# A two-layer decoder on one core: more buffers for routed pages, and new engine orders for its last stage

## The chip, the cores and the metric
The kernel runs on one core of a Trainium2 chip. The time is that of the device for one execution, in microseconds (us); three runs of the kernel before gave 4082.57 (median), 4074.16 and 4083.14. One more execution was profiled. The core has five engines with instruction queues of their own: TensorE (PE), VectorE (DVE), ScalarE (ACT), GpSimd (POOL) and SyncE (SP), which only issues DMAs. Each runs its queue in order; semaphores tie them together.

## The reference
A decoder of two layers works on 4096 tokens (64 sequences of 64) with 128 features, all in float32. A second input of the same shape, the context, is used by the cross attentions.

```python
x = x + L0_attn(ln(x))           # delta rule attention, 4 heads      stage A
x = x + L0_xattn(ln(x), ctx)     # cross attention, 16 heads          stage B
x = x + L0_ffn(ln(x))            # 6 layers: local attention + FFN    stage C
x = x + L1_attn(ln(x))           # cosine attention, 16 heads         stage D
x = x + L1_xattn(ln(x), ctx)     # gated attention, 8 heads           stage E
x = x + L1_ffn(ln(x))            # mixture of experts                 stage F
```

In the last step each token is sent to 3 of 16 experts. An expert computes relu(x W1 + b1) W2 + b2 with a hidden width of 256; its result is weighted by the gate. The three results are added to the token.

## The kernel before
**Tiles and stages.** The tokens lie in 32 tiles of 128. Stage A+B ("ab"), stage C ("c") and stage D+E with the routing of F ("de") each run over the tiles as a software pipeline. A unit is one tile in one stage, and each unit consists of named items per engine. Stage C runs 6 layers over the 32 tiles, and after every four tiles a feed-forward unit C2; its last one (layer 5, group 7) ends the stage.

**Orders.** `DE_ORDER` holds for each engine the order of one slot. In `"G5 t4 T3"` the letters are the item and the last digit (base 36) is the lag: in slot n the engine runs item `G` of unit n-5, then `t` of unit n-4, then `T` of unit n-3. `schedule` gives every item a due time, BEGIN[stage][engine] + SLOT[stage] * (slot + place / items), and sorts all stages' items by it. So a stage's SLOT and BEGIN decide only how its items interleave with those of the neighbouring stages; within a stage the order is what `DE_ORDER` says. Waits are on semaphores and come from the data flow, whatever the order.

**Items of stage "de".** `st1`, `ag1`, `n1`, `r1`, `xn1` normalise the tile; `X1` transposes it, `J` is the projection to queries, keys and values; `sq`, `ln`, `lx`, `qn` scale them, `T` transposes, `s` (scores), `c0`, `c1` (clipping, DVE), `e0`, `e1` (exp, ACT), `p0`, `p1` (transposes), `u`, `n`, `t`, `w` (weighted values and output). The gated attention has `xc`, `g`, the gates' small items on DVE and ACT up to `cs`, `gb` (POOL, L1992), `G` (PE, two banks), `dm` and `mx` (DVE), `d2` (POOL, L1884), `ex` (ACT), `C` (DVE, L1369), `ct`, `av`, `hh` to `h4`, `h5`, `h6` (POOL) and `x`. The routing has `X3`, `g3`, `ti` to `cu` on DVE, `rk`, `gT`, `b2`, and `sc`: three scatters (POOL, L2021) of the tile's rows into the experts' lists in HBM (`xg`).

**Banks.** PE's results go to eight PSUM banks in turn (`take` in `build`); an item waits until whoever reads the bank's earlier result is done with it. `G`, `s` and `u` take two banks.

**Pages.** A page is 128 rows of one expert's list, with the expert's weights. There are 111. `FT` units (DVE) make tables of pages once 8, 12, 16, 20, 24, 28 and 32 tiles are routed; SP's `blocks` reads them and issues for each page two loads, of rows and their weights and targets (`XB`, 65 KB, L623) and of the expert's matrices (`FW`, 257 KB, L624). Page j runs through `T`, `h`, `o` on PE, `T`, `h` on ACT, `o` on DVE (result into `YB`), `zz` on POOL (scatter to `zg`, L2030). Pages 0 to 68 run inside the stage, three per slot from unit 9 on (`BT0`, `Bh0`, `Bo0` and so on; `Bz` on POOL); for earlier units PE runs filler matmuls (`fill`) in their places. Pages 69 to 110 come after it in the tail (`FB_ORDER`), then SP loads the results back and DVE and POOL add them.

**Places.** `XB` and `FW` have 8 places (`NXB`), `YB` has 4 (`NYB`). SP may load page j when PE has done `o` of page j-8 and the scatter of page j-8 has landed, since the scatter reads its targets from `XB`. DVE's `o` of page j waits for the scatter of page j-4.

**Activation tables.** ACT's `table` loads another set when an item needs it: gelu for the items `g0` to `g2` of C2, exponentials and logarithms for most of stage "de". Copies and squares need none.

Of the kernel before, what the change touches and what calls it, by code (L numbers as in the profile page):

```python
# [23 lines left out]
PAGES = (3 * TOK + NE * 127) // 128  # L24
XROWS = NE * CAP + PAGES * 128
ZROWS = 3 * TOK + (NE + PAGES) * 128
NXB, NYB = 8, 4
STEPS = [(t, 3 * t - 15) for t in range(8, NT, 4)] + [(NT, PAGES)]
# [4 lines left out]
def shape_constants():  # L33
# [14 lines left out]
    for k in range(5):  # L48
# [58 lines left out]
DE_ORDER = {  # L107
# [8 lines left out]
}  # L116
# [22 lines left out]
for _kind in "12":  # L139
# [7 lines left out]

SLOT = {"ab": 13.426, "c": 11.263, "de": 14.030, "fb": 1.2, "fc": 3.0}
BEGIN = {
    "ab": {"pe": 0.0, "act": -19.77, "dve": -27.0, "pool": -23.98},  # L150
    "c": {"pe": 448.83, "act": 425.56, "dve": 432.24, "pool": 458.45},
    "de": {"pe": 3221.92, "act": 3186.93, "dve": 3246.05, "pool": 3263.81},
}
# [93 lines left out]
def build(nc, din, out, stages=("A", "B", "C", "D", "E", "F"), depth=DEPTH):  # L247
    with ExitStack() as ctx:
# [11 lines left out]
        WB = sb("WB", [128, OF + 1066 + 128])  # L260
# [31 lines left out]
        tables = WB[0:1, 532:532 + 128 * len(STEPS)].bitcast(I32)  # L292
        FW = [WB[:, 1428 + 514 * p:1942 + 514 * p] for p in range(NXB)]
        XB = [WB[:, 5540 + 130 * p:5670 + 130 * p] for p in range(NXB)]
        YB = [WB[:, 6580 + 128 * p:6708 + 128 * p] for p in range(NYB)]
        XT = [WB[:, 7092 + 128 * p:7220 + 128 * p] for p in range(4)]
        HID = [WB[:, 7604 + 256 * p:7860 + 256 * p] for p in range(4)]
        xg = nc.dram_tensor("xg", (XROWS, 130), F32, kind="Internal").ap()
# [69 lines left out]
        names += ["wat0", "wat1", "wq", "wf", "out", "rt", "empty", "const", "rope", "ones", "blank", "prime", "half", "shift"]  # L368
        names += [f"xr{i}" for i in range(3)] + [f"bw{i}" for i in range(NXB)]
        names += [f"ys{i}" for i in range(NYB)] + ["lists", "seen"]  # L370
# [174 lines left out]
        def _(eng):  # L545
# [63 lines left out]
            def blocks():  # L609

                for s in qkv_free(depth - 1) + [uC2[(depth - 1, 7)].on("pe", "o")]:
                    w.wait_ge(*s)
                for k, u in enumerate(FT):
                    for p in range(3):
                        w.wait_ge(f"xr{p}", 48 * len(range(p, u.at["t"], 3)))
                    w.wait_ge(*u.on("dve", "v"))
                    for j in range(u.at["first"], u.at["n"]):
                        if j >= NXB:
                            w.wait_ge(*FB[j - NXB].on("pe", "o"))
                            w.wait_ge(f"ys{(j - NXB) % NYB}", 16 * ((j - NXB) // NYB + 1))  # L620
                        c = 128 * k + j - u.at["first"]
                        at = eng.value_load(tables[0:1, c:c + 1], min_val=0, max_val=XROWS - 128)
                        eng.dma_start(XB[j % NXB], xg[bass.ds(at, 128), :]).then_inc(sems[f"bw{j % NXB}"], 16)  # L623
                        eng.dma_start(FW[j % NXB], din["F_W"][bass.ds((at >> 12) * 128, 128), :]).then_inc(sems[f"bw{j % NXB}"], 16)  # L624

# [44 lines left out]
            w.wait_ge("rt", 16)  # L670
            for i in range(NXB):
                w.wait_ge(f"bw{i}", 32 * len(range(i, PAGES, NXB)))

# [4 lines left out]
        def _(te):  # L678
# [393 lines left out]
            def pe_fb(u, ph):  # L1072
                j = u.at["j"]
                for v, e, m in u.after[ph]:
                    w.wait_ge(*v.on(e, m))
                K, W = bank[u.bank[ph]], FW[j % NXB]
                if ph == "T":
                    w.wait_ge(f"bw{j % NXB}", 32 * (j // NXB + 1))
                    o = tr(K[:, 0:128], XB[j % NXB][:, 0:128])
                elif ph == "h":  # L1080
                    w.wait_ge(f"bw{j % NXB}", 32 * (j // NXB + 1))
                    w.wait_ge(*u.on("act", "T"))
# [12 lines left out]
        def _(se):  # L1095
# [241 lines left out]
            def act_fb(u, ph):  # L1337
                j = u.at["j"]
                K, W = bank[u.bank[ph]], FW[j % NXB]
                w.wait_ge(*u.on("pe", ph))  # L1340
# [4 lines left out]
                elif ph == "h":  # L1345
                    w.wait_ge(f"bw{j % NXB}", 32 * (j // NXB + 1))
                    if j >= 4:
# [9 lines left out]
        def _(ve):  # L1357
# [522 lines left out]
        def _(pe_):  # L1880
# [220 lines left out]
```

## Time and profile before

| what | value |
|---|---|
| runs, median of three | 4082.57 us |
| profiled execution | 4061.49 us |
| its span, first to last instruction | 4059.7 us |
| granted TensorE clock, mean | 0.961 of full |
| PE busy | 3798.1 us, 94% |
| DVE, ACT, POOL busy | 81%, 78%, 66% |
| stage "de" | about 3260 to 3940 us |
| tail: the last 42 pages, results, output | about 3940 to 4060 us |

The page cuts the span into 40 slices of 101.5 us. A digit of a slice is the busy share in tenths; in the line PEclk it is the clock granted to TensorE. In rows of instructions, `ps<-BIG` is what is written and read, and `[1.34 <-DVE BIG L1369]` says that the engine was idle for 1.34 us before it and that this instruction of VectorE ended the wait. `x8` is a count; a float32 matmul stands as two records. Most items share the lines of a few helpers (L682 matmul, L686 transpose, L1361, L1369, L1372 on DVE, L1099 and L1107 on ACT, L1884 on POOL), so they are told apart by their shapes and tiles.

### The profile page before, as it was taken

To read this page: it belongs to the slowest core of one execution; us is meant where nothing else is said; L and a number is where in the kernel's file an instruction comes from. 1 tells how busy PE (TensorE), PEld (TensorE's weight loads), DVE (VectorE), ACT (ScalarE), POOL (GpSimd) and SP (SyncE) were. 2 spreads that over 40 slices of the span, in tenths; PEclk is the share of its full clock that TensorE was granted. 3 is DMA by queue.
4 is the path that set the end of the run, shared out by engine and by line. 5 is a ranking of instruction groups with operands and counts; after the bars stand their busy time and mean duration, and the time that the engine had idled before them with its cause. 6 is when DMAs were issued, how large, how long until landed. Compare 5 with 4: busy or idle time off the path is not lost.

```text
span 4059.7 us, 143038 instructions
## 1 busy us (share of the span) xinstructions
PE 3798.1 (94%) x58268; PEld 2739.9 (67%) x58268; DVE 3285.5 (81%) x9302; ACT 3182.2 (78%) x9278; POOL 2692.5 (66%) x2319
## 2 busy tenths in 40 slices
PE   7999989999999999999999999999999978888873
PEld 5767756666676766766666766767666757667663
DVE  4666699998989999898889989898999847766642
ACT  3555579899999999999899999999998946656642
POOL 3444487887777777777777777777777714344444
PEclk9999999999999999999999999999999989977868
DMA  3000000000211111111201121111110000122246
GB/s 110 4 4 5 5 2 4 5 5 5 47 19 26 26 31 36 24 26 26 52 14 26 26 44 30 17 26 26 52 39 9 10 10 16 54 67 70 70 111 203
DMA packets 168664, 139.87 MB, mean 34 GB/s; under 512 B 37076, under 2 KB 148744, under 8 KB 167032
## 3 DMA queue, kind: packets, MB, share of 16 engines
q1 hardware_dynamic: 161384, 117.04, 12.9%
q0 software_dynamic: 6624, 13.68, 1.0%
q8 instruction: 461, 7.55, 0.8%
q14 instruction: 195, 1.60, 0.1%
HBM read 108.72 MB, written 57.23 MB: 41 GB/s over the span
## 4 chain that ended last, share of the span: by engine, by line
PE 71%; DVE 15%; ACT 8%; issue 4%; DMA 1%; POOL 1%; SPq 0%; DVEq 0%; another core or an unknown queue 0%; POOLq 0%; ACTq 0%
PE ps L682 55%; PE ps L686 16%; DVE BIG L1361 7%; ACT BIG L1107 5%; DVE sm L1372 3%; ACT BIG L1099 2%; DVE BIG L1369 1%; POOL sm L1887 1%; DVE sm L1361 1%; DMA zg<-WB 1%; DVE x_sb L1361 0%; DMA WB<-in_F_W 0%; DVE BIG L1503 0%; DVE sm L1543 0%; DVE WB L1365 0%
## 5 line engine op out<-in xcount | busy, mean ns | idle before, releaser
L1099 ACT ACTIVATE BIG<-ps 128x512 f32<-128x512 f32 (+5 forms) x2784 | 1450.8, 575 | 405.7 <-PE ps L686 235.4
L682 PE MATMUL ps<-WB,BIG 128*128 128x128 f32 (+2 forms) x6528 | 1682.1, 391 | 4.9 <-DVE BIG L1361 1.8
L1884 POOL TENSOR_TENSOR BIG<-BIG,sm 128x512 f32<-128x512 f32 (+1 forms) x864 | 1214.7, 1430 | 673.1 <-DVE sm L1543 305.2
L686 PEld LDWEIGHTS ps<-t_ident,BIG 128*128 128x128 f32 x5952 | 717.4, 144 | 486.2 <-issue 299.3
L1884 POOL TENSOR_TENSOR BIG<-BIG 128x512 f32<-128x512 f32 x776 | 972.8, 1280 | 87.4 <-DVE BIG L1361 72.4
L686 PE MATMUL ps<-t_ident,BIG 128*128 128x128 f32 x5952 | 914.4, 281 | 75.4 <-DVE BIG L1369 38.6
L682 PEld LDWEIGHTS ps<-WB,BIG 128*128 128x128 f32 (+1 forms) x6528 | 863.2, 192 | 174.3 <-issue 153.5
L1372 DVE TENSOR_REDUCE sm<-BIG 128x8 f32<-128x512 f32 (+5 forms) x1440 | 857.1, 623 | 6.9 <-ACT BIG L1107 5.2
L682 PEld LDWEIGHTS ps<-BIG 64*64 64x64 f32 (+2 forms) x37888 | 605.0, 128 | 321.6 <-issue 145.5
L682 PE MATMUL ps<-BIG 64*64 64x64 f32 (+4 forms) x37888 | 728.6, 222 | 62.8 <-ACT BIG L1107 18.1
L1107 ACT ACTIVATE BIG<-ps,sm 128x64 f32<-128x64 f32 (+1 forms) x3104 | 700.6, 394 | 37.7 <-DVE sm L1372 35.8
L1361 DVE TENSOR_TENSOR BIG<-ps,rc 128x512 f32<-128x512 f32 x768 | 525.6, 684 | 144.1 <-ACT BIG L1107 137.5
L1107 ACT ACTIVATE BIG<-ps 128x512 f32<-128x512 f32 (+1 forms) x832 | 496.2, 627 | 133.7 <-PE ps L682 119.0
L1361 DVE TENSOR_TENSOR BIG<-ps,rs 128x256 f32<-128x256 f32 x1536 | 570.9, 412 | 0.0
L1372 DVE TENSOR_REDUCE sm<-ps 128x8 f32<-128x512 f32 (+1 forms) x416 | 263.6, 643 | 113.0 <-PE ps L682 81.3
L1887 POOL TENSOR_TENSOR sm<-sm,halfn 128x1 f32<-128x1 f32 (+2 forms) x208 | 187.5, 902 | 206.2 <-DVE sm L1365 84.8
L682 PE MATMUL ps<-BIG,WB 128*128 128x512 f32 (+2 forms) x608 | 295.4, 577 | 1.4 <-ACT BIG L1107 1.4
L1099 ACT ACTIVATE ps<-t_bandm 128x512 f32<-128x512 f32 x384 | 233.4, 697 | 0.0
L1107 ACT ACTIVATE sm<-sm 128x32 f32<-128x32 f32 (+2 forms) x672 | 152.8, 232 | 65.0 <-DVE sm L1365 58.3
L682 PEld LDWEIGHTS ps<-BIG,WB 128*128 128x128 f32 (+2 forms) x608 | 104.2, 176 | 119.4 <-issue 83.5
L2030 POOL DMA_INDIRECT zg<-WB x111 | 109.3, 985 | 113.4 <-DVE WB L1365 83.3
L682 PE MATMUL ps<-WB 128*128 128x128 f32 (+1 forms) x926 | 170.3, 327 | 6.0 <-ACT WB L1107 3.0
(152 smaller groups left out, 3557.1 us busy)
## 6 DMA issues: line engine op xcount, KB each, us to landing
xg<-in_F_empty SPq DMA_DIRECT2D x64, 520.0 KB, 8.1
WB<-in_F_W SPq DMA_DIRECT2D x111, 257.0 KB
WB<-in_Wqkv SPq DMA_DIRECT2D x6, 1536.0 KB, 7.5
WB<-xg SPq DMA_DIRECT2D x111, 65.0 KB
xg<-in_F_empty SPq DMA_DIRECT2D x6, 1040.0 KB, 7.6
BIG<-zg SPq DMA_DIRECT2D x8, 768.0 KB, 10.0
XS<-y_sb SPq DMA_DIRECT2D x96, 63.0 KB
y_sb<-in_ctx SPq DMA_DIRECT2D x16, 256.0 KB, 3.8
```

The source lines that it names most:

```text
L682: return te.matmul(o, l, r, start=start, stop=stop, skip_group_check=not check)
L686: return te.transpose(o, i, ident[0:n, 0:n])
L1099: return se.activation(o, i, ACT.Copy)
L1107: return se.activation(o, i, f, **kw)
L1361: return ve.tensor_tensor(o, a, b, op)
L1369: return ve.scalar_tensor_tensor(out=o, in0=a, scalar=s, in1=b, op0=op0, op1=op1)
L1372: return ve.tensor_reduce(o, a, AX, op, negate=negate)
L1884: return pe_.tensor_tensor(o, a, b, op)
L1887: return pe_.tensor_tensor(o, a, halfn[:, 0:n], ALU.pow)
L2030: pe_.indirect_dma_start(zg[:, :], bass.IndirectOffsetOnAxis(ap=XB[j % NXB][:, 128:129].bitcast(U32), axis=0), YB[j % NYB], None).then_inc ...
```

## The change
Three things change. The places: `XB` gets 16 and moves from `WB` to the free end of `BIG`, `YB` gets 12, `FW` keeps its 8 under the name `NFW`. SP now waits for PE's `o` of page j-8, and for the scatter of page j-16; DVE's `o` waits for the scatter of page j-12. The four orders of stage "de" are others, with the same items. And the stage's slot is 13.846 instead of 14.030, with other begins, so that more of its items come before the last ones of stage C: 14 on PE instead of 4, 9 on ACT instead of 1, 34 on DVE instead of 15.

```diff
-NXB, NYB = 8, 4
+NFW, NXB, NYB = 8, 16, 12
...
 DE_ORDER = {
-    "pe": "g37 av6 X13 p04 Bh19 cs5 Bo09 J3 BT29 u4 rk7 Bo19 Bh29 G5 t4 T3 w4 Bo29 s3 gT7 BT08 xc4 ct5 b27 Bh08 om5 g4 "
-           "X36 BT18 p13",
-    "act": "lx6 n49 r49 Bh2c t7 T6 ex8 r15 n27 r27 gTa BT0b xc7 n39 r39 e16 ct8 X39 e06 Bh0b g17 BT1b x39 g27 em8 X15 "
-           "p16 p06 vc5 Bh1b n14 xr9 BT2b sq5 h28 ln5",
-    "dve": "mm4 st23 h45 s36 gg6 ix6 ag23 og6 Bo28 C4 xn23 x5 c12 st35 ag35 c02 st10 xn35 xn11 ge3 cu6 b26 md4 ab3 ag10 "
-           "m35 ti5 ls3 id5 a04 cf5 a14 oh5 a24 gs5 a34 mb5 cs3 a44 gj3 hh4 a1 s14 Bo07 v1 h24 ss1 su5 rk5 n01 r2 v14 n2 "
-           "sl5 gm5 qn1 Bo17 dm3 mx3 w2 gr5",
-    "pool": "Bz17 Bz27 gb2 id4 Bz06 d22 bo0 h53 h63 sc4",
+    "pe": "t2 G3 T1 Bh16 w2 Bo06 s1 Bh26 X34 xc2 ct3 g34 Bo16 om3 g2 X10 Bo26 av3 rk4 p01 cs2 p11 BT05 gT4 J0 u1 Bh05 "
+           "BT15 b24 BT25",
+    "act": "n35 n23 r35 r23 Bh17 X35 xc3 Bh27 x35 ct4 e02 xr5 g13 em4 g23 e12 X11 p02 n10 p12 gT5 BT06 r10 sq1 h24 ln1 "
+           "n44 lx1 t2 r44 vc2 Bh06 BT16 BT26 T1 ex3",
+    "dve": "ss5 n6 n05 v18 b29 cu9 qn5 h48 dm7 mx7 x8 st38 xn14 w6 mm7 st13 ag38 st26 ag26 C7 xn38 xn26 c05 Bo0a c15 m38 "
+           "ti8 su8 id8 gs8 ge6 cf8 gm8 ab6 oh8 md7 gr8 mb8 Bo1a Bo2a ls6 a07 gg8 a17 ag13 rk8 og8 cs6 a27 sl8 gj6 a37 "
+           "s38 a47 ix8 hh7 s17 a4 v4 h27 r5",
+    "pool": "id5 gb3 sc5 h54 h64 d23 Bz07 bo1 Bz17 Bz27",
...
-SLOT = {"ab": 13.426, "c": 11.263, "de": 14.030, "fb": 1.2, "fc": 3.0}
+SLOT = {"ab": 13.426, "c": 11.263, "de": 13.846, "fb": 1.2, "fc": 3.0}
...
-    "de": {"pe": 3221.92, "act": 3186.93, "dve": 3246.05, "pool": 3263.81},
+    "de": {"pe": 3243.70, "act": 3231.50, "dve": 3186.74, "pool": 3234.79},
...
-        XB = [WB[:, 5540 + 130 * p:5670 + 130 * p] for p in range(NXB)]
-        YB = [WB[:, 6580 + 128 * p:6708 + 128 * p] for p in range(NYB)]
+        XB = [BIG[:, 23250 + 130 * p:23380 + 130 * p] for p in range(NXB)]
+        YB = [WB[:, 5540 + 128 * p:5668 + 128 * p] for p in range(NYB)]
...
                     for j in range(u.at["first"], u.at["n"]):
+                        if j >= NFW:
+                            w.wait_ge(*FB[j - NFW].on("pe", "o"))
                         if j >= NXB:
-                            w.wait_ge(*FB[j - NXB].on("pe", "o"))
                             w.wait_ge(f"ys{(j - NXB) % NYB}", 16 * ((j - NXB) // NYB + 1))
```

## Rows read from the trace of the kernel before

**Rows 1.** The page's slices of the span: TensorE busy and granted clock, tenths.
```profile
PE   7999989999999999999999999999999978888873
...
PEclk9999999999999999999999999999999989977868
```

**Rows 2.** Stretches: us, busy PE, PEld (weights), DVE, ACT, POOL, clock, DMA share, GB/s.
```profile
3400.00:3450.00 50.00, 44.23 (x644) 36.32 (x642) 40.53 (x190) 33.02 (x116) 20.69 (x30) 1.00 0.05 17
...
3950.00:4000.00 50.00, 29.23 (x216) 24.68 (x215) 8.41 (x24) 21.63 (x72) 23.24 (x25) 1.00 0.70 190
```

**Rows 3.** Chain of waits, 3400 to 3500 us: start, length, engine and line.
```profile
3436.60 4.16 PE ps L682 x88
...
3452.37 4.17 PE ps L682 x88
```

**Rows 4.** Chain of waits, 3600 to 3800 us, the same columns.
```profile
3747.45 3.41 PE ps L682 x12
...
3767.62 3.42 PE ps L682 x12
```

**Rows 5.** Timeline of TensorE (start, length, count, idle before), slot without pages.
```profile
3462.15 0.29 PE L686 MATMUL ps<-t_ident,BIG 128*48 128x128 f32 x1 [1.34 <-DVE BIG L1369]
```

**Rows 6.** Timeline of TensorE, a slot with pages: before `s`, before `gT`, in `av`.
```profile
3736.34 1.09 PE L682 MATMUL ps<-BIG 32*64 32x256 f32 x16 [0.48 <-ACT BIG L1107]
...
3738.94 0.29 PE L686 MATMUL ps<-t_ident,BIG 128*48 128x128 f32 x1 [1.51 <-DVE BIG L1369]
...
3745.78 0.40 PE L682 MATMUL ps<-V,BIG 64*64 64x17 f32 x3 [0.56 <-issue]
```

**Rows 7.** Timeline of VectorE, the same slot with pages: `mx` and `C`.
```profile
3734.89 0.69 DVE L1372 TENSOR_REDUCE sm<-BIG 128x8 f32<-128x512 f32 x1
...
3738.22 0.67 DVE L1369 SCALAR_TENSOR_TENSOR BIG<-ps,BIG 128x512 f32<-128x512 f32 x1
```

**Rows 8.** Table of stretches, ten microseconds each, in slots with pages.
```profile
3690.00:3700.00 10.00, 7.90 (x138) 6.27 (x138) 9.71 (x37) 6.77 (x27) 5.08 (x7) 1.00 0.18 47
...
3700.00:3710.00 10.00, 10.00 (x73) 8.53 (x75) 5.52 (x43) 5.43 (x20) 4.35 (x6) 0.50 0.10 31
```

**Rows 9.** Timeline of SyncE in the tail: issues of page loads (L623 rows, L624 weights).
```profile
3930.68 0.33 SPq L623 DMA_DIRECT2D WB<-xg  x1
...
3968.72 0.33 SPq L623 DMA_DIRECT2D WB<-xg  x1
...
3970.44 0.33 SPq L623 DMA_DIRECT2D WB<-xg  x1
...
4017.97 0.34 SPq L623 DMA_DIRECT2D WB<-xg  x1
```

**Rows 10.** Chain of waits in the tail, 3900 to 4060 us.
```profile
3981.22 3.98 DMA zg<-WB
...
3990.34 2.79 DMA WB<-in_F_W
```

**Rows 11.** Timeline of GpSimd: the last scatter of results.
```profile
4027.53 0.97 POOL L2030 DMA_INDIRECT zg<-WB  x1 [0.30 <-issue]
```

**Rows 12.** DMA queues, 3950 to 4020 us: packets, MB, share of sixteen engines.
```profile
q1 hardware_dynamic: 9525, 10.93, 60.8%
...
q0 software_dynamic: 1065, 2.16, 8.3%
```

**Rows 13.** Timeline of TensorE at the stage's begin: the first transpose of unit 0.
```profile
3276.63 0.41 PE L686 MATMUL ps<-t_ident,BIG 128*128 128x128 f32 x1 [4.65 <-DVE BIG L1366]
```

**Rows 14.** Timeline of ScalarE at the stage's begin: a table load and what follows it.
```profile
3271.00 1.28 ACT L1114 ACT_TABLE_LOAD   x1
...
3272.30 0.29 ACT L1107 ACTIVATE sm<-mv,eps 128x1 f32<-128x1 f32 x1
```

**Rows 15.** Timeline of GpSimd, a slot without pages: `gb`, then `d2`.
```profile
3453.41 0.61 POOL L1992 COPY BIG<-sm 128x512 f32<-128x512 f32 x1 [3.46 <-DVE sm L1361]
...
3459.13 1.04 POOL L1884 TENSOR_TENSOR BIG<-BIG,sm 128x512 f32<-128x512 f32 x1 [4.79 <-DVE sm L1372]
```

More of the change, by code:

```diff
@@ L292, in build @@
         tables = WB[0:1, 532:532 + 128 * len(STEPS)].bitcast(I32)
-        FW = [WB[:, 1428 + 514 * p:1942 + 514 * p] for p in range(NXB)]
-        XB = [WB[:, 5540 + 130 * p:5670 + 130 * p] for p in range(NXB)]
-        YB = [WB[:, 6580 + 128 * p:6708 + 128 * p] for p in range(NYB)]
-        XT = [WB[:, 7092 + 128 * p:7220 + 128 * p] for p in range(4)]
-        HID = [WB[:, 7604 + 256 * p:7860 + 256 * p] for p in range(4)]
+        FW = [WB[:, 1428 + 514 * p:1942 + 514 * p] for p in range(NFW)]
+        XB = [BIG[:, 23250 + 130 * p:23380 + 130 * p] for p in range(NXB)]
+        YB = [WB[:, 5540 + 128 * p:5668 + 128 * p] for p in range(NYB)]
+        XT = [WB[:, 7076 + 128 * p:7204 + 128 * p] for p in range(4)]
+        HID = [WB[:, 7588 + 256 * p:7844 + 256 * p] for p in range(4)]
         xg = nc.dram_tensor("xg", (XROWS, 130), F32, kind="Internal").ap()
@@ L368, in build @@
         names += ["wat0", "wat1", "wq", "wf", "out", "rt", "empty", "const", "rope", "ones", "blank", "prime", "half", "shift"]
-        names += [f"xr{i}" for i in range(3)] + [f"bw{i}" for i in range(NXB)]
+        names += [f"xr{i}" for i in range(3)] + [f"bw{i}" for i in range(NFW)]
         names += [f"ys{i}" for i in range(NYB)] + ["lists", "seen"]
@@ L622, in blocks @@
                         at = eng.value_load(tables[0:1, c:c + 1], min_val=0, max_val=XROWS - 128)
-                        eng.dma_start(XB[j % NXB], xg[bass.ds(at, 128), :]).then_inc(sems[f"bw{j % NXB}"], 16)
-                        eng.dma_start(FW[j % NXB], din["F_W"][bass.ds((at >> 12) * 128, 128), :]).then_inc(sems[f"bw{j % NXB}"], 16)
+                        eng.dma_start(XB[j % NXB], xg[bass.ds(at, 128), :]).then_inc(sems[f"bw{j % NFW}"], 16)
+                        eng.dma_start(FW[j % NFW], din["F_W"][bass.ds((at >> 12) * 128, 128), :]).then_inc(sems[f"bw{j % NFW}"], 16)
             def results():
@@ L670, in _ @@
             w.wait_ge("rt", 16)
-            for i in range(NXB):
-                w.wait_ge(f"bw{i}", 32 * len(range(i, PAGES, NXB)))
+            for i in range(NFW):
+                w.wait_ge(f"bw{i}", 32 * len(range(i, PAGES, NFW)))
         c_again = 32 if "C" in stages else 16
@@ L1075, in pe_fb @@
                     w.wait_ge(*v.on(e, m))
-                K, W = bank[u.bank[ph]], FW[j % NXB]
+                K, W = bank[u.bank[ph]], FW[j % NFW]
                 if ph == "T":
-                    w.wait_ge(f"bw{j % NXB}", 32 * (j // NXB + 1))
+                    w.wait_ge(f"bw{j % NFW}", 32 * (j // NFW + 1))
                     o = tr(K[:, 0:128], XB[j % NXB][:, 0:128])
                 elif ph == "h":
-                    w.wait_ge(f"bw{j % NXB}", 32 * (j // NXB + 1))
+                    w.wait_ge(f"bw{j % NFW}", 32 * (j // NFW + 1))
                     w.wait_ge(*u.on("act", "T"))
@@ L1338, in act_fb @@
                 j = u.at["j"]
-                K, W = bank[u.bank[ph]], FW[j % NXB]
+                K, W = bank[u.bank[ph]], FW[j % NFW]
                 w.wait_ge(*u.on("pe", ph))
@@ L1345, in act_fb @@
                 elif ph == "h":
-                    w.wait_ge(f"bw{j % NXB}", 32 * (j // NXB + 1))
+                    w.wait_ge(f"bw{j % NFW}", 32 * (j // NFW + 1))
                     if j >= 4:
@@ L1853, in dve_fb @@
                 j = u.at["j"]
-                w.wait_ge(f"bw{j % NXB}", 32 * (j // NXB + 1))
+                w.wait_ge(f"bw{j % NFW}", 32 * (j // NFW + 1))
                 w.wait_ge(*u.on("pe", "o"))
@@ L2027, in pool_fb @@
                 j = u.at["j"]
-                w.wait_ge(f"bw{j % NXB}", 32 * (j // NXB + 1))
+                w.wait_ge(f"bw{j % NFW}", 32 * (j // NFW + 1))
                 w.wait_ge(*u.on("dve", "o"))
```

## The prediction

> **What bounds the kernel now.** I read the page's slices first: TensorE (PE) is busy nine tenths or more up to the 32nd slice, then eight tenths at a clock of 0.6 to 0.9 of full, and at the very end it idles [rows 1]. So stages A to C (0 to 3260 us) are left alone by the diff, and what counts is the routed stage, 3250 to 3940, and the tail, 3940 to 4060.
>
> In the routed stage the table of stretches shows PE busy 44 of 50 us at full clock around 3400, where no pages are in yet [rows 2]. The chain of waits repeats its longest piece once per token tile: every 15.8 us in the first part [rows 3], every 20.2 us in the second [rows 4]. The difference is mostly the clock, since the first part runs filler matmuls in the places of the pages' own. PE's timeline shows where it idles: in each slot once before `gT`, 1.34 us without pages [rows 5], 1.51 us with them, after 0.48 us before the scores `s` [rows 6]. The releaser is VectorE (DVE) L1369, which is item `C`: `gT` takes the PSUM bank that `G` filled eight banks earlier, and that is free when `C` has read it. From `mx` (DVE, 3734.89) to `C` (3738.22) pass 3.3 us, with DVE busy on ten other items [rows 7]. The ten microseconds that end with such a stall run at full clock, the next ten at 0.50, the lower level (1.2 GHz instead of 2.4) [rows 8]. Such a half-clock stretch came once in nearly every slot with pages, and in none of the slots at 15.8 us.
>
> In the tail the last 42 pages go through. SyncE (SP) issues their two loads; from page 69's (3930.68) to page 110's (4017.97) are 41 steps of 2.13 us on average [rows 9]. Yet where SP has not to wait, a step takes 1.72 us (3968.72 to 3970.44). The chain there goes scatter (`DMA zg<-WB`, 3.98 us), SP, weight load (2.79 us), PE, and back to a scatter [rows 10]: SP may reload a place only when the scatter of the page eight before has landed.
>
> **The tail, part by part.** XB gets 16 places, so the landing of a scatter is asked of page j-16; the weight place FW[j-8] is free once PE has done `o` of page j-8, which comes about five microseconds of scatter sooner. YB has 12 places, so DVE's `o` waits on the scatter of j-12 instead of j-4. The instructions are the same in number; what goes is waiting.
> What is late next? The loop through FW: a page's `o` comes three pages after its `T` on PE, then about 1.2 us of PE work, 1.3 us of SP, 2.8 us of landing [rows 10]: 8P = 3P + 5.3, P = 1.06 us; with a landing of 5 us, 1.5 us. GpSimd (POOL) sends a scatter every 1.27 us [rows 11]. The DMA engines carry 60.8% + 8.3% of 70 us for 34 pages [rows 12], 1.42 us per page. PE has 29.2 us of work in 50 us, or 24 pages [rows 2]: 1.2 us. All are under SP's own step, so P = 1.72 to 1.76; I take 1.74. 41 x (2.13 - 1.74) = 16.0 us. At the end the last scatter leaves POOL at 4027.5, 0.30 us behind the one before it and so out of a queue [rows 11]; with pages 1.74 apart and scatters 1.27 apart the queue is gone: 1 us more. The first of these loads stays tied to the last routing table, which moves with the stage. Tail: -17, bounds -25 (DMA's 1.42 as P, +4 of landing) and -5 (P = 2.0, as DMA sets it when scatters and loads collide).
> The Trainium skill (DMA: Bandwidth & Descriptors, Issuing engines are not separate DMA queues) says the issuing sequencer's time is usually small relative to the DMA. By it the tail would go to the DMA engines' 1.42 us and win 29 us. Here the issue step is the longest of all, so I go by the row.
>
> **The begin.** Today unit 0's `xn1` (DVE L1366) waits for `r1`, which stands on ScalarE (ACT) behind `g2` of the last feed-forward group, and PE sits idle 4.65 us before its transpose at 3276.6 [rows 13]. In the new order `st1`, `ag1`, `xn1` of unit 0 go right behind that group's `tr`, and `X1`, `J` between its `g1` and `g2` on PE. Against that ACT now alternates: gelu set, exponential set, gelu, exponential, before unit 0's squares; counted off the order it has seven loads where it had three, the first hidden while ACT waits. A load costs 1.28 us and the next activation starts 0.02 us later [rows 14]. By hand, with the durations of the rows: ACT's `T` of unit 0 is only some 1 us earlier, `c0`/`c1` 3 to 5, the transposes `p` 5 to 7 because the last group's output matmul (5 us at half clock) now stands behind them. By due times the whole unit is 12 to 16 us earlier, which ACT will not allow. I take -5, bounds +2 and -13. What is late next is ACT.
> The Trainium skill (ScalarE: Activation LUTs, What ACT_TABLE_LOAD costs) adds a drain of about 1.4 us to each load, 2.66 us in all. With it four more loads would cost 10.6 us and the begin would win nothing. The rows show no such pause.
>
> **The slots.** I placed the new PE order on the banks. `G` is still followed by five bank takers (`T`, a page's `h`, `w`, a page's `o`, `s`), and now `Bh2` waits for `C`. So the stall stays. Between `mx` and `C` DVE has nine items, by their durations 2.4 us, where it had 2.6, and no page result any more: `C` comes 0.2 us sooner, in slots with pages 0.2 sooner again. PE has a page's `h` (0.6 us) between where `t` (0.45) stood, and the 0.48 before `s` goes since `T` comes first behind `G`. So the idle time falls from 1.7 to about 1.4 in the 12 slots without pages and from 2.0 to 1.5 in the 16 with them, of which something will come back elsewhere: -0.3 x 12 - 0.4 x 16 = -10. The planner's slot shrinks 14.030 to 13.846, 1.3%; of the 15.8 and 20.2 measured that is 0.2 and 0.26 a slot, or -7. Bounds: 0 (POOL, below) and -18. This assumes the half-clock stretches stay as they are.
> POOL is the queue that is moved: the three scatters of `sc` stand now between `gb` and `d2`, with `h5`, `h6`. From the end of `gb` (3454.0) to `d2` (3459.1) are 5.1 us [rows 15]; PE has 1 us more work in that span in the new order, and POOL needs 3 x 1.27 + 1.2 = 5.0. It fits by 1 us without pages; with pages, two page scatters come before `gb` and it fits just so. Late by 0.5 us it would cost 8 us over 16 slots.
>
> **The depth.** By due times (begin + slot x (lag + place/items)) a unit took 85.1 us from `st1` to `cu`, now 80.8. The stage's end comes that much sooner: 4.3, stretched up to 1.4 times as the slots are: -5, bounds -3 and -8.
>
> **Sum.** -17 - 5 - 10 - 5 = -37 us. The profiled execution took 4061.49 (span 4059.7 and 1.8 around it), so it would become 4024.5. It lies 21 us under the median of 4082.57; taken off the median it gives 4045.
>
> **Rivals.** (1) The clock holds. The stall with pages becomes what the stall without pages is, 1.3 us, and those slots never fell. Against it: PE also starves by 0.4 to 0.6 us at a time in the `av` matmuls, with nothing waited for [rows 6], and the half-clock stretch began there too; where that falls in new code can't be read. If half of the 16 slots keep full clock: 8 x 4.4 = 35 more, 4010; all, 3975.
> (2) The tail is held by DMA: P = 1.9. Then it wins 10, and the time is 4052.
> (3) The places bring nothing, since FW still has eight: P stays 2.13, the tail wins 1, the time is 4061. Against it speak the 3.98 us of scatter in the chain.
> (4) Slower: the stall grows instead. If POOL's `sc` makes `d2`, and so `C`, late in slots without pages too, they stall as the slots with pages do, after whose 1.51 us the clock was at half. Then the 12 slots at 15.8 cost what the 16 cost: 12 x 4.4 = +53, and the ten won in the slots are lost: 4082.6 - 27 + 53 = 4108. It decides as soon as `sc` and `h6` end after `mx`. For it: 1 us of room only. Against: in these slots no page scatters run.
>
> **How the numbers follow.** Forecast 0.50 (own range 4030 to 4062), (1) 0.22, (2) 0.10, (3) 0.06, (4) 0.10, the new order worth nothing and the tail as forecast (4065) 0.02. 0.3%, about what a measurement of this kernel can tell from no change, is 12 us. All but (4) are faster by more; of their far ends I give 0.03 to same: faster 0.87, same 0.03, slower 0.10. The range takes the forecast, (2), (3), the half case of (1): 3985 to 4072.
>
> **What would show it.** SP's steps at 1.72 to 1.76 in the tail, with hardly a scatter in its waits; four more table loads around 3270 and `xn1` some ten microseconds sooner; one PE stall per slot, now ahead of a page matmul and not `gT`, of 1.3 us; slots of 15.5 and 19.8. Wrong it is if the clock's digits between the 32nd and 38th slice change, up or down, if POOL's `d2` no longer follows `mx` at once, or if SP's steps stay over 1.9.

## The result, and the profile after

The kernel after takes 4100.2 us (median, 4082.6 to 4112.2) beside 4076.8 us (4060.3 to 4098.8) for the kernel before: ratio 1.0057, interval 1.0042 to 1.0071. It is slower by 0.6%, where the forecast said 0.9% faster. The profiled execution took 4100.2 us (span 4098.4), 38.7 us over that of before.

The page's slices of after, to be read beside [rows 1]: the clock is a tenth or two lower in the 33rd to 35th slice, where the slots without pages lie (8, 9, 9 before; 7, 8, 7 now), and a tenth higher in the 36th and 37th.

```profile
PE   7999989999999999999999999999999888888874
...
PEclk8999999999999999999999999999999978788867
```

Stretches of after (us, busy time of PE, PEld, DVE, ACT, POOL, clock, DMA share, GB/s). The first answers to the first of [rows 2]: PE has 527 matmul records in 50 us where it had 644, at 0.81 of the clock instead of 1.00; DVE does 29.7 us of work instead of 40.5.

```profile
3400.00:3450.00 50.00, 43.18 (x527) 34.06 (x526) 29.73 (x141) 22.97 (x86) 16.93 (x24) 0.81 0.04 14
```

Where the 38.7 us are (from the start of PE's `J` in each tile to the next): the first `J` comes 2.0 us sooner and the next four slots together 1.6. The twelve after them, up to the first slot of full pages, last 250 us instead of 196: +54. Most of them take 19.7 us where they took 15.8. The fifteen left take 303 us instead of 313: -10. From the last `J` to the last `b2` it is 7 us more, and from the last `b2` to the end 127.3 us instead of 135.6: -8.3.

So everything hangs on twelve slots (one of them, 25.8 us where it was 16.5, is longer than the rest). DVE's timeline shows two of them, 19.66 us apart, at item `r`, the reciprocal that waits for PE's `u`. Each begins with four idle microseconds whose releaser the trace doesn't know:

```profile
3465.39 0.26 DVE L1654 RECIPROCAL sm<-ps 128x16 f32<-128x16 f32 x1 [4.03 <-remote]
...
3485.05 0.26 DVE L1654 RECIPROCAL sm<-ps 128x16 f32<-128x16 f32 x1 [3.99 <-remote]
```

PE's timeline in that slot. `u` is 64 small matmuls (64x9). They start at 3480.06 and run dense for half a microsecond, then stutter with nothing waited for. The recorded end of the last (3482.82) isn't the end of the work: the semaphore that it raises, and with it `r`, comes at 3485.0. After it `t` waits 1.31 us for DVE, and the granted clock is at half, 1.2 GHz, from 3485.4 to 3492.2.

```profile
3480.06 1.41 PE L683 MATMUL ps<-V,BIG 64*64 64x9 f32 x58
3481.92 0.30 PE L683 MATMUL ps<-V,BIG 64*64 64x9 f32 x5 [0.45 <-issue]
3482.65 0.17 PE L683 MATMUL ps<-V,BIG 64*64 64x9 f32 x1 [0.43 <-issue]
...
3485.83 0.48 PE L683 MATMUL ps<-t_ident,BIG 128*64 128x128 f32 x3 [1.31 <-DVE BIG L1362]
```

POOL's timeline beside it: the three scatters of `sc`, which the change put behind `gb`, lie exactly over `u`.

```profile
3479.18 0.61 POOL L1993 COPY BIG<-sm 128x512 f32<-128x512 f32 x1 [5.31 <-DVE sm L1362]
3480.59 1.07 POOL L2022 DMA_INDIRECT xg<-BIG  x1 [0.79 <-ACT BIG L1100]
3481.97 0.95 POOL L2022 DMA_INDIRECT xg<-BIG  x1 [0.30 <-issue]
3483.22 0.96 POOL L2022 DMA_INDIRECT xg<-BIG  x1 [0.30 <-issue]
...
3490.22 1.10 POOL L1885 TENSOR_TENSOR BIG<-BIG,sm 128x512 f32<-128x512 f32 x1 [1.86 <-DVE sm L1373]
```

In the kernel before, the same `u` met no scatter in these slots:

```profile
3454.28 1.12 PE L682 MATMUL ps<-V,BIG 64*64 64x9 f32 x64
```

And in its slots with pages the collision was there all along, on `av` (32 small matmuls, 64x17), of which [rows 6] hold the last line. From the kernel before, three more lines of PE's timeline and, under them, two of POOL's:

```profile
3742.96 0.99 PE L682 MATMUL ps<-V,BIG 64*64 64x17 f32 x27
3744.33 0.27 PE L682 MATMUL ps<-V,BIG 64*64 64x17 f32 x1 [0.39 <-issue]
3745.04 0.18 PE L682 MATMUL ps<-V,BIG 64*64 64x17 f32 x1 [0.44 <-issue]
```

```profile
3742.52 0.96 POOL L2030 DMA_INDIRECT zg<-WB  x1 [0.30 <-issue]
3743.78 0.96 POOL L2030 DMA_INDIRECT zg<-WB  x1 [0.31 <-issue]
```

The time of a burst, from its first matmul to the semaphore of its last, tells more than the records between. Over the whole stage:

```
kernel   burst  without a scatter   with scatters over it (mean)
before   av     12x, 1.13 us        20x, 2.72 us, with 1.20 us of scatters over it
after    u       3x, 1.15 us        29x, 4.84 us, with 2.86 us of scatters over it
after    av     27x, 1.13 us        none
                 5x, 1.92 us (at half clock)
```

On average that is 1.3 us for each microsecond of scatter, in both. In before a part of it is the clock: six of the 20 `av` bursts ran wholly at half clock, where `av` takes 1.92 us without any scatter, and took 1.92 to 3.29 us. At full clock it is 3.13 us with 1.50 over it (3617.38), again 1.3 for each. (The Trainium skill, Perfetto Trace Analysis, section DMA Instruction — SWDGE (GPSIMD), says that such a row ends when the last descriptor is written, not when the data has moved; so what is counted here as overlap is the making of descriptors. The traces agree that the data moves after the row: in e6, below, the scatter's row ends 1.60 us after the start of `u`, and its packets begin at 2.17.)

### The profile page after: what moved, and what is told of

Read it like the earlier page. It is cut to its first block, busy times and chain, and to the rows that moved or that the text cites. A ratio compares the mean times of both kernels' runs of the same rounds, so it can differ in the third digit from the quotient of the medians.

```text
span 4098.4 us, 142970 instructions
## 1 busy us (share of the span) xinstructions
PE 3829.4 (93%) x58268; PEld 2763.0 (67%) x58268; DVE 3275.9 (80%) x9302; ACT 3168.9 (77%) x9282; POOL 2691.0 (66%) x2319
## 4 chain that ended last, share of the span: by engine, by line
PE 67%; DVE 17%; ACT 7%; issue 4%; another core or an unknown queue 3%; POOL 1%; SPq 1%; DMA 1%; DVEq 0%; POOLq 0%; ACTq 0%
PE ps L683 52%; PE ps L687 15%; DVE BIG L1362 7%; ACT BIG L1108 5%; DVE sm L1373 3%; ACT BIG L1100 2%; DVE BIG L1370 1%; DVE BIG L1367 1%; DVE x_sb L1362 1%; POOL sm L1888 1%; DMA WB<-in_F_W 0%; DVE BIG L1504 0%; POOL BIG L1885 0%; SPq L623 0%
## 5 line engine op out<-in xcount | busy, mean ns | idle before, releaser
L687 PEld LDWEIGHTS ps<-t_ident,BIG 128*128 128x128 f32 x6063 | 741.7, 146 | 479.5 <-issue 305.6
L687 PE MATMUL ps<-t_ident,BIG 128*128 128x128 f32 x6063 | 965.4, 285 | 62.3 <-DMA WB<-in_F_W 19.7
L683 PE MATMUL ps<-BIG 64*64 64x64 f32 (+4 forms) x37888 | 743.3, 224 | 52.4 <-issue 16.0
L683 PEld LDWEIGHTS ps<-WB 128*128 128x128 f32 (+1 forms) x926 | 148.6, 232 | 47.0 <-issue 20.5
```

What stands on the lines that cost most here:

```text
L683: return te.matmul(o, l, r, start=start, stop=stop, skip_group_check=not check)
L687: return te.transpose(o, i, ident[0:n, 0:n])
```

## The experiments

Theory C: a scatter on POOL slows a burst of small matmuls that it overlaps. Theory L is the prediction's rival (4): the scatters make `d2`, and so `C`, late. Theory O: the new PE order loses the clock by itself. Scatters over a burst are called the collision. Each run stands beside runs of the kernel before on the same chip; the chips turned out to matter.

```
chip  run                            us (median)  before   ratio (95%)
 8    e1 sc behind d2                4055.5       4068.3   0.9965 (0.9948 to 0.9983)
 8    e2 sc waits for u              4111.9       4068.3   1.0102 (1.0079 to 1.0126)
 8    e3 old orders, sc on u         4145.0       4068.3   1.0184 (1.0159 to 1.0208)
 8    e4 places alone                4060.6       4068.3   0.9970 (0.9950 to 0.9990)
 0    e5 page scatters spread        4044.3       4075.0   0.9921 (0.9897 to 0.9944)
 0    e6 one scatter on u            4065.7 (one run)      4075.0
 0    e7 tensor work on u            4060.2 (one run)      4075.0
 0    e8 plain DMAs on u             4051.7 (one run)      4075.0
14    e9 old orders, spread          4022.4       4034.3   0.9967 (0.9948 to 0.9987)
14    e10 bo ahead of sc             3980.9       4034.3   0.9870 (0.9838 to 0.9902)
14    e11 and sc waits for X3        3978.2       4034.3   0.9859 (0.9821 to 0.9896)
14    e12 orders alone               4013.9 (one run)      4034.3
 7    e13 after itself               3982.5       4036.3   0.9872 (0.9836 to 0.9908)
 7    e14 orders alone               4003.6       4036.3   0.9917 (0.9889 to 0.9945)
 7    e15 = e10                      3983.2       4036.3   0.9877 (0.9844 to 0.9911)
 7    e16 = e11                      3983.9       4036.3   0.9862 (0.9824 to 0.9901)
15    e17 = e10                      4052.1       4076.3   0.9936 (0.9909 to 0.9963)
15    e18 = e11                      4108.6       4076.3   1.0085 (1.0058 to 1.0112)
```

**e1, the scatters moved off `u`.**

```
-    "pool": "id5 gb3 sc5 h54 h64 d23 Bz07 bo1 Bz17 Bz27",
+    "pool": "id5 gb3 h54 h64 d23 sc5 Bz07 bo1 Bz17 Bz27",
```

> The kernel after, with POOL's `sc` (three scatters) moved from behind `gb` to behind `d2`: "id5 gb3 h54 h64 d23 sc5 Bz07 bo1 Bz17 Bz27". Theory C (collision): in the trace of after, the 64 matmuls of `u` take 1.15 us where POOL issues nothing and 5.0 us where its three scatters (2.99 us of them) lie over them, in 26 of 31 slots; DVE's `r` waits 4.0 us for them, then ACT and PE wait for DVE, and the granted clock falls. Moved away, `u` takes 1.15 us again in every slot without pages, these slots go from 19.7 us back to 15.5 to 16, and 10 of them give 37 to 42 us; slots with pages give something too, so 4010 to 4060 us. Theory L (POOL's `sc` makes `d2` and so `C` late, the prediction's rival): faster as well, by up to 40 us, with `d2` starting sooner behind `mx`. Theory O (PE's new order in itself loses the clock, whatever POOL does): within 5 us of 4100, slots of 19.7 us stay.

One token of POOL's order turned 1.0057 into 0.9965 (each against before on its own chip). `u` is dense again, DVE's `r` follows it, and the slot is 15.4 us (3424.78 to 3440.17), under the 15.8 of before. In e1's timelines of PE and DVE, the stall that is left is the one forecast, 1.42 us ahead of filler `Bh2`, on `C` (the releaser named is DVE's L1370, which is `C` in this kernel):

```profile
3423.60 1.12 PE L683 MATMUL ps<-V,BIG 64*64 64x9 f32 x64
...
3432.25 0.71 PE L683 MATMUL ps<-t_ident 128*128 128x128 f32 x4 [1.42 <-DVE BIG L1370]
```

```profile
3424.78 0.26 DVE L1654 RECIPROCAL sm<-ps 128x16 f32<-128x16 f32 x1 [0.19 <-PE ps L683]
...
3440.17 0.26 DVE L1654 RECIPROCAL sm<-ps 128x16 f32<-128x16 f32 x1 [0.19 <-PE ps L683]
```

Theory O is out for these slots: PE's order is that of after. With pages the train of six scatters now reaches `av` (14 times 3.82 us, with 1.79 over it), and these slots stay at 20 us.

**e2, the scatters held back instead.**

```
+                    if u.at["t"] + 3 < NT:
+                        w.wait_ge(*DE[u.at["t"] + 3].on("pe", "u"))
```

> The kernel after, order unchanged, but POOL's `sc` of tile t waits for PE's `u` of tile t+3 (the one that its scatters lay over), so that it begins when these 64 matmuls are over, and still lies ahead of `h5`, `h6` and `d2`, now about 1.2 us later. Theory C: `u` takes 1.15 us in every slot, slots without pages 15.5 to 16.5 us, total 4010 to 4060 us, within 10 us of the run with `sc` behind `d2`. Theory L: the scatters are still between `gb` and `d2` and later than before, so nothing is won, 4095 to 4120 us. Theory O: 4095 to 4110 us.

The time is that of theory L, 4111.9, and 52 us over C's range, yet the trace doesn't show L. `u` took 1.16 us, as C says, and `d2` follows `mx` at once (3487.50 + 0.69, 3488.26). The scatters, from 3482.5 to 3486.1, fell on the next burst, the 16 matmuls of `G`'s scores: in the 26 slots where that burst ran at full clock it took 2.57 us on average instead of 0.71, with 1.68 us over it. In e2's timeline of DVE, `dm`, which waits for `G`, has the same unknown releaser:

```profile
3486.77 0.69 DVE L1362 TENSOR_TENSOR BIG<-ps,t_causm 128x512 f32<-128x512 f32 x1 [2.27 <-remote]
3487.50 0.69 DVE L1373 TENSOR_REDUCE sm<-BIG 128x8 f32<-128x512 f32 x1
```

The slots without pages went to 17 to 22 us. So C covers `G` too. L has a price only where POOL is late for `d2`, and it was so in two slots of this run (by 1.1 us behind `mx` at 3350.39 and by 0.8 at 3862.06), once in e12 (0.5 us), and in no slot of the others, after among them.

**e3, the collision put into the kernel before.**

```
-    "pool": "Bz17 Bz27 gb2 id4 Bz06 d22 bo0 h53 h63 sc4",
+    "pool": "Bz17 Bz27 gb2 sc5 id4 Bz06 d22 bo0 h53 h63",
```

> The kernel before with one token of POOL's order moved: `sc` stands behind `gb` (as in after) and so comes under PE's `u`: "Bz17 Bz27 gb2 sc5 id4 Bz06 d22 bo0 h53 h63". PE's, ACT's and DVE's orders are the old ones. Theory C: `u` goes from 1.16 us to 3 to 5 us in the slots without pages, these go from 15.8 us to 18 to 20 us (12 of them: +26 to +48 us); in slots with pages `av` is freed of half its scatters, so the total is 4070 to 4110 us, that of after without its better tail. Theory L: `d2` is 4 to 5 us behind `gb` anyway and the three scatters last 3.6 us, so it isn't late: 4055 to 4070 us. Theory O: the old PE order keeps its clock in the slots without pages: 4055 to 4070 us.

4145 us, past the upper end of C's own range, and 75 over what L and O allow. `u` took 4.4 us without pages and 5.9 with them (a page's scatter, `Bz0`, now queues behind `sc`, so 3.9 us lie over it), and the slots 19.4 to 25 us. The old orders of PE, ACT and DVE are in place here and the slots stretch all the same, which settles O.

**e6, the dose; e7 and e8, what in a scatter does it.** In e6 one scatter stays under `u` and two stand behind `d2`. In e7 and e8 all three stand behind `d2`, and in their old place POOL does other work, added to the kernel:

```
# e7, cut to its main lines
+                elif ph == "sd":
+                    idle = WB[:, 8640:9152]
...
+                    for i in range(3):
...
+                            pe_.tensor_tensor(idle, idle, idle, ALU.add).then_inc(sems["idle"], 1)
# e8, cut to its main lines
+                elif ph == "sd":
+                    for i in range(3):
...
+                        pe_.dma_start(nul[r:r + 128, :], T["D_W"][:, 0:130]).then_inc(sems["idle"], 16)
```

> A dose: one of `sc`'s three scatters stays where after has it (under `u`), the other two stand behind `d2`. Theory C with a price by the microsecond of overlap (5.0 - 1.15 over 2.99 us = 1.3): `u` takes 2.2 to 2.6 us, slots without pages 16.3 to 17.2 us, 4065 to 4085 us. Rival (any scatter costs PE a fixed stall or the clock): `u` 4 us or more, or slots of 19 us or more.

> All scatters behind `d2`; in their old place under `u` POOL does three tensor operations of 128x512 on a spare stretch of SBUF (1.04 us each by the row of `d2`). What does a scatter do to PE: if it is POOL's traffic with SBUF, `u` takes 3 to 5 us again and the slots 18 to 20 us; if it is the issue of an indirect DMA (its descriptors) or its transfer, `u` takes 1.15 us and the slots without pages stay at 15.4 to 16 us (4051 to 4065 us).

> All scatters behind `d2`; in their old place under `u` POOL issues three plain DMAs of the same size (128 rows of 520 bytes, SBUF to a spare DRAM tensor). If it is the transfer that slows PE, `u` takes 2.5 us or more in the slots without pages; if it is POOL's making of the descriptors of an indirect DMA, `u` takes 1.15 us and the slots stay at 15.4 to 16 us. DVE, ACT and PE do the same work as in the run with `sc` behind `d2` (4051.5 us span).

e6: `u` 2.15 us with 1.07 over it (0.9 us for each microsecond, a little under what was expected), slots of 16.5. The data of this scatter moves too late to be the cause: its row on POOL lies 0.53 to 1.60 us behind the start of `u`, and its first packet comes 2.17 us behind it, as `u` ends. In e6's DMA view of 3446 to 3450 us, 0.1 us a digit, the scatter's packets are in the 23rd to 25th digit, from 3448.28 on (the 3 ahead of them is a packet of instructions); `u` ran from 3446.12 to 3448.29:

```profile
3446.65 1.07 POOL L2022 DMA_INDIRECT xg<-BIG  x1 [0.80 <-ACT BIG L1100]
```

```profile
DMA  0000000000030000000000194000000000000000
```

In e7 and e8 the other work covers `u`, and `u` doesn't feel it; slots 15.4 us in both. POOL's and PE's timelines of e7:

```profile
3431.57 3.30 POOL L2021 TENSOR_TENSOR WB<-WB 128x512 f32<-128x512 f32 x3
```

```profile
3431.87 1.11 PE L683 MATMUL ps<-V,BIG 64*64 64x9 f32 x64
```

The same two of e8:

```profile
3430.27 1.75 POOL L2019 DMA_DIRECT2D nul<-t_D_W  x3
```

```profile
3430.59 1.11 PE L685 MATMUL ps<-V,BIG 64*64 64x9 f32 x64
```

The plain DMAs went through the same software queue (672 packets on q0 in 50 us, 352 without them). In the slot shown only 22 of their 96 packets fell on `u`, but in one with pages, at 3664.40, 77 did, and `u` took 1.16 us there too. So neither tensor work of POOL nor transfers of that size do it, nor does POOL's issue of plain DMAs; what does is POOL's work on an indirect one, before its data moves. What in that work slows PE is not settled.

**e4, the places alone** (after with the old DE orders, slot and begins).

> The kernel after with the old DE orders, slot and begins: only the 16 places for rows and 12 for results are new. The prediction's terms say that the places bring the depth term and part of the tail: 4040 to 4058 us (at most one page's DMA sooner for each of 42 pages in the tail). Rival (places bring nothing, SP's step is the floor): 4056 to 4066 us. Neither theory on the slots says anything of this run: slots as in before.

4060.6 us is 2.6 over the range given from the prediction's terms and within the rival's. Yet the places bring something. The tail takes 122.2 us from the last `b2` against 135.6, 13.4 less, at 1.71 us a page against 1.97. Of this the medians show 8: in the profiled execution half-clock stretches fell into a few slots without pages, for which no run gives a cause.

**e5, the page scatters moved off `av`.**

```
+    "pool": "id5 Bz18 gb3 Bz28 h54 h64 d23 sc5 Bz07 bo1",
```

> The run with `sc` behind `d2`, and two of the three page scatters of a slot moved from behind `bo` to both sides of `gb`: "id5 Bz18 gb3 Bz28 h54 h64 d23 sc5 Bz07 bo1". With `sc` behind `d2` alone, the slots with pages lasted 20.2 us and their `av` (32 small matmuls) 4.1 us instead of 1.13, with 1.95 us of scatters over it. Theory C: without them `av` takes 1.1 to 1.9 us, the slots with pages 17 to 18.5 us, 16 to 20 of them give 30 to 50 us: 4005 to 4028 us. Rival (slots with pages are held by the clock or by PE's own work of some 17 us at half clock, and `av` is only where it shows): slots of 19.5 to 20.5 us, 4048 to 4060 us.

C's direction, a third of its size. `av` met scatters for half a microsecond or more 9 times instead of 14, and slots with pages take 18 to 22 us. A third burst is hit now, the 16 matmuls of `s`: three times 2.0 us instead of 1.14, with 1.0 us over them, and once 3.1 with 2.2. The longest stall is another one. In PE's timeline of e5 a page's matmul (`Bh2`) can't start for 2.19 us behind `s`, while `sc` runs on POOL from 3768.52. That looks like a collision and isn't: `s` raised its semaphore 1.13 us after its start, as without scatters, and `Bh2` starts when DVE's `C` ends, at 3770.85.

```profile
3767.62 1.09 PE L683 MATMUL ps<-BIG 32*64 32x256 f32 x16 [0.37 <-ACT BIG L1108]
3770.91 0.71 PE L683 MATMUL ps<-WB 128*128 128x128 f32 x4 [2.19 <-issue]
```

```profile
3770.17 0.68 DVE L1370 SCALAR_TENSOR_TENSOR BIG<-ps,BIG 128x512 f32<-128x512 f32 x1
```

It is the stall that the prediction placed there, longer in the slots, every fourth, in which DVE also makes a page table: `C` then starts 3.7 us after `mx` and not 2.8. The same stall lasts 2.24 us in a slot of e1 without pages (3463.95), and 2.20 us in e10, on a chip where the collision is nearly free; there the trace names the releaser:

```profile
3592.52 0.71 PE L683 MATMUL ps<-WB 128*128 128x128 f32 x4 [2.20 <-DVE BIG L1370]
```

In e5 the stretch behind it ran wholly at the lower clock level, 1.2 GHz:

```profile
3772.00:3792.00 20.00, 19.12 (x177) 15.93 (x178) 10.40 (x57) 9.37 (x36) 5.27 (x9) 0.50 0.34 97
```

**e9 to e12: another chip.** e9 is e4 with the page scatters behind `id`; e10 and e11 are e5 with `bo` ahead of `sc`, and with a wait of `sc` for PE's `X3`; e12 is the kernel before with the new orders alone. The expectations of e10 and e11 read the stall of e5 ahead of `Bh2` as a collision.

```
+    "pool": "gb2 id4 Bz17 Bz27 Bz06 d22 bo0 h53 h63 sc4",        # e9
+    "pool": "id5 Bz18 gb3 Bz28 h54 h64 d23 bo1 sc5 Bz07",        # e10, e11
+                        w.wait_ge(*DE[u.at["t"] + 1].on("pe", "X3"))     # e11, before the scatters
```

> Old orders with the new places, and POOL's two page scatters that lie under `av` moved behind `id`: "gb2 id4 Bz17 Bz27 Bz06 d22 bo0 h53 h63 sc4". In the run with the places alone `av` took 3.2 us in the slots with pages (1.5 us of scatters over it), and these slots 20.2 us. Theory C: `av` keeps at most the last of `sc`'s scatters (0 to 0.6 us over it), 1.13 to 1.9 us; `u` may get 0.8 us of one; slots with pages 18 to 19.5 us, 4020 to 4048 us. Rival (the slots with pages are set by PE's own work at half clock): 20 us, 4055 to 4064 us as with the places alone. Against the new orders with the same cure (4044 us) it tells what the new orders are worth once the collision is gone: by the prediction 0.3 to 0.4 us a slot, 5 to 11 us.

> New orders with the page scatters spread, and `bo` (0.46 us) between `d2` and `sc`: "id5 Bz18 gb3 Bz28 h54 h64 d23 bo1 sc5 Bz07". In the spread run PE stood 2.2 us ahead of a page's matmul, right behind the 16 matmuls of `s`, while the first scatter of `sc` ran, and its clock fell there. Theory C2 (any burst of small matmuls is hit, `s` too, in its first 0.5 us after the burst): the stall is shorter in part of the slots, 4030 to 4043 us. Rival (0.5 us is too little, the stall is the matmul's own wait): 4040 to 4048 us.

> As the run with `bo` ahead of `sc`, and `sc` of tile t also waits for PE's `X3` of tile t+1, which stands behind `s` and the page's matmuls `Bh2`: the scatters begin when that burst and its followers are over, some 1 to 3 us later. Theory C2: no stall of 1 us or more ahead of the page's matmuls (`ps<-WB`) in the slots with pages; the clock holds longer there; 4015 to 4040 us, unless the last scatters now reach `av` (then 4040 to 4055 us, with `av` at 2 to 4 us).

> The kernel before with the new orders, slot and begins, but the old 8 places for rows and 4 for results. If the parts of the change add up, it has after's slots (19.7 us) and before's tail (135.6 us from the last `b2` to the end against 127.3): 4105 to 4112 us in the profiled execution. If the places are needed for the new orders to work, it is slower than that.

Only e9 falls into its range, and not for the reason given there; the other three lie 37 to 91 us under theirs. The reason is one: on chip 14 the kernel before itself takes 4034 us, not 4068 to 4077, and the collision is nearly free. e12 has after's orders, with `sc` over `u`; `u` took 1.39 us with 0.88 over it, and most slots were 15.1 to 15.5 us, with pages too (21.8 where a table is made). e9 to e11 can't test C there, since their cure treats what the chip hasn't got.

**e13 to e18: the same kernels on more chips.**

> The kernel after, unchanged, beside the kernel before. Theory H (the collision depends on the chip): if this chip is like the one of the last four runs (before near 4034 us), `u` takes 1.2 to 1.5 us, slots 15.2 to 15.5 us, and after is faster than before: 3980 to 4005 us; if it is like the others (before near 4070 us), `u` takes 5.0 us and after 4085 to 4110 us. Theory K (the old places spare the new orders the collision): `u` takes 5.0 us here whatever the chip.

> New orders with the old places, once more. Theory H: `u` as in the kernel after itself on the same chip, 1.2 to 1.5 us or 5.0 us; total 8 to 20 us over after itself (the tail of the old places). Theory K: `u` at 1.4 us and slots of 15.2 us on any chip, 4005 to 4020 us.

> New orders, page scatters spread, `bo` ahead of `sc`, once more. Theory H: on a chip with the collision 4025 to 4045 us (slots with pages 17 to 21 us where the scatters meet `s`, `av` or the page's matmuls), on one without it 3975 to 3990 us. Theory K: 3975 to 3990 us on any chip.

> The same with `sc` waiting for `X3`, once more. Theory H: on a chip with the collision between 4010 and 4045 us, on one without it 3970 to 3990 us. Theory K: 3970 to 3990 us on any chip.

> New orders, page scatters spread, `bo` ahead of `sc`, a third time. On a chip with the collision (before near 4070 us): the same scatters as in the spread run (4044 us there) but 0.5 us later behind `s`, so 4030 to 4045 us; slots with pages 15.5 to 22 us. On a chip without it (before near 4035 us): 3978 to 3990 us as before, slots of 15.2 us.

> The same with `sc` waiting for `X3`. On a chip with the collision: the scatters miss `s` and the page's matmuls but their last one reaches `av` (0.83 us over it where pages are few), so `av` takes 2 us instead of 1.13 in every slot; 4010 to 4045 us. On a chip without it: 3968 to 3992 us.

The kernel after, unchanged, is 1.3% faster than before on chip 7, as theory H said. Its scatters stand in the same place (POOL's timeline of e13), and DVE's `r` comes 1.39 us after the start of `u` at 3500.00, 0.2 us later than without them in e1. The slots with pages take 15.1 us (3639.36 to 3654.47; every fourth, with a table, 21.8), where the profile on which the prediction rests had 20.2. Of its slots without pages six took 17.1 us, at a clock of 0.90 to 0.92, as in e14 (0.91); e12, the kernel of e14 on chip 14, had 15.5 at 1.00 there, and no run gives a cause:

```profile
3500.53 1.07 POOL L2022 DMA_INDIRECT xg<-BIG  x1 [0.80 <-ACT BIG L1100]
```

```profile
3501.39 0.26 DVE L1654 RECIPROCAL sm<-ps 128x16 f32<-128x16 f32 x1 [0.39 <-PE ps L683]
...
3639.36 0.26 DVE L1654 RECIPROCAL sm<-ps 128x16 f32<-128x16 f32 x1 [0.40 <-PE ps L683]
3654.47 0.26 DVE L1654 RECIPROCAL sm<-ps 128x16 f32<-128x16 f32 x1 [0.39 <-PE ps L683]
```

The sharpest pair is e11 and e18, one kernel on two chips. In a slot without pages POOL's second scatter begins 0.44 us ahead of `av` on chip 14 (3427.68, 3428.12) and 0.43 us ahead on chip 15 (3419.04, 3419.47). DVE's `a0`, which waits for `av`, starts 1.16 us after the start of `av` on the one (DVE's timeline of e11, first line) and 2.74 us after on the other (the same of e18):

```profile
3429.28 0.17 DVE L1694 COPY sm<-ps 128x8 f32<-128x8 f32 x1 [0.52 <-PE ps L683]
```

```profile
3422.21 0.17 DVE L1694 COPY sm<-ps 128x8 f32<-128x8 f32 x1 [2.10 <-remote]
```

The whole is 1.4% faster than before on chip 14 and 0.9% slower on chip 15. There e18 lies 64 us over its range, since not one scatter but most of the train reached `av` (30 times, 4.13 us with 2.39 over it); e17 lies 7 us over its own, and e14 is 21 us over e13 where 8 to 20 were expected.

Theory K is out: e13, with the new places, has `u` at 1.40 us, and e14, the same orders with the old ones, behaves alike on the same chip. Chips 8, 0 and 15 have the collision in every kernel that was profiled there, and on 14 and 7 it costs a burst at full clock 0.4 us or less (mostly 0.2) in all of them; the profiled executions of before and after that the result rests on had it. The kernel before has a profile on no numbered chip: there its kind is read from its time alone (4068 to 4076 us, or 4034 to 4036). Whether a chip keeps its kind over time was not tried, and what differs between them stays open. Of the three kernels that ran on both kinds, after, that of e10, e15 and e17, and that of e11, e16 and e18, the second alone is faster than before on each: 0.9936 where the collision is and 0.987 to 0.988 where it isn't. e5 had 0.9921 on chip 0 and was not run on the other kind.

## Why the prediction was wrong

**The step that failed** is the one on POOL in "The slots". It named the right move (three scatters between `gb` and `d2`) and weighed it against one thing only, whether `d2` still gets its turn. It does: in after, `d2` (3490.22) follows `mx` (3489.45 + 0.69) at once, and so it does in every slot of after. What lay on the other side of the move, PE's `u` under the scatters, wasn't asked. Measured, it cost 3.9 us in most of the 12 slots and +54 us in all, where the forecast had them 0.3 us shorter each. The price stood in rival (4) all the same: 12 x 4.4 = +53 there, with 4108 forecast for 4100 measured. That it fits is luck. The rival had the queue and the slots, and the wrong victim; e2 shows that a run can even hit its number while its mechanism doesn't act.

**The sign stood in a row that was read past.** The `av` gaps of [rows 6], "with nothing waited for", were taken as a nuisance that can't be placed, and the slots with pages [rows 4] as slow by the clock [rows 8]. In fact `av` took 2.72 us on average there, with 1.20 us of scatters over it; POOL's timeline beside PE's, not shown in the rows, would have told it. On chips 14 and 7, without that, slots with pages run at 15.1 us in the new order. The clock falls behind these stalls and adds to their cost. Not all half clock comes from scatters: in the new order it also follows the stall on `C` where a table is made (e10, no collision: 0.69 from 3593.5 to 3610).

**Slots with pages**: forecast -0.4 us x 16, measured -10 over fifteen. Right in sign. Two things lie in it that the forecast had not: `av` was freed of scatters in every slot (1.13 us), and `u` got them. **Slots without**: forecast -0.3 each. On the kernel with `sc` out of the way (e1) 15.4 instead of 15.8: right, and the stall is where it was put. `C` starts 2.85 us after `mx` in after, where it was 3.32: more than the 0.2 us forecast. But where DVE makes a table it is 4.02, a case that the forecast left out. The new orders were worth 0.8% by themselves where the collision is absent (e14).

**Tail**: forecast -17, measured -8.3. The waits for scatters are gone from SP, and where it has not to wait a step takes 1.72 us, as said (3981.30 to 3983.02 in after's timeline):

```profile
3981.30 0.33 SPq L624 DMA_DIRECT2D BIG<-xg  x1
...
3983.02 0.33 SPq L624 DMA_DIRECT2D BIG<-xg  x1
```

But the forecast made that the average, 1.74. Over the same 41 steps, from page 69's load to page 110's, SP took 1.92 us in after (3979.16 to 4057.76), 1.86 in e4 and 1.83 in e13, where before had 2.13. That is past the 1.9 which the prediction gave as a sign of being wrong, and 41 x 0.21 = 8.7 us comes near what the tail won. The base is soft as well: counted at DVE's results, before had 1.97 us a page, not 2.13, since SP issued page 69's loads 13 us ahead of its result and page 110's 6.5 us ahead. By that count after has 1.80, and e4, e2 and e13 have 1.71. What sets SP's longer steps in after is open.

**Begin**: forecast -5. The first `J` came 2.0 us sooner, tile 0's `xn1` 6.5 us (3269.64 instead of 3276.14; about ten were forecast), its `b2` 9.3 by the semaphore that it raises. Four table loads more, as counted off the order (eight from 3240 to 3330, four before). **Depth**: forecast -5; it was +7 from the last `J` to the last `b2`, since a unit's length stretches with the slots. Without the collision that stretch is 70.6 us (e13, e14), where before had 72.2 and after 79.1.

**On chip 7** all terms act at once, and after wins 54 us on a forecast of 37. That chip's kernel before has no profile here, so the 17 between them aren't split. There, on a kind of chip that the profile of before had not come from, the direction would have been right, and the size half as large again.

## What to carry to other kernels

Before a DMA with computed addresses is moved on GpSimd's queue, look at what TensorE does in the microseconds it moves onto: here bursts of 16 to 64 small matmuls paid about a microsecond or more for each microsecond of it (0.9 in e6, 1.3 in after) on three of five chips. A gap "with nothing waited for", or a wait whose releaser the trace doesn't know, is to be laid beside the other engines' timelines before it is called noise, or a collision: the stall of e5 was a plain wait for DVE. And a verdict of half a per cent for an order of work can hang on the chip: the same two kernels gave 1.0057 and 0.9872.

## What was not expected of the hardware

- Three indirect scatters (2.99 us) over 64 small matmuls make 1.15 us into 5.0. `av`, `G` and `s` are hit too: `G`'s 0.71 us became 2.57 with 1.68 over it (e2), and the 1.14 of `s` 3.1 with 2.2 over it (e5). Three tensor operations of 1.1 us or three plain DMAs of the same bytes in that place cost nothing. It acts before the scatter's data moves (e6).
- It is a matter of the chip: in the same kernel `u` takes 1.40 us with 0.89 over it on chip 7, and 4.84 with 2.86 in the execution profiled for the result.
- The trace's own records of PE mislead in such a burst: the last of 64 matmuls is recorded as over 2.2 us before its semaphore moves, so the waiting engine's row is the one to read.
